# A decoder layer of 32 batches: one value run of sixteen heads a batch, new loop orders, rows of ones by transfers

## The reference

```python
# 1 self attention with a threshold
probs = softmax(x @ x.T / 16);  vac = where(probs < 0.01, probs, 0)
sparse = where(probs < 0.01, 0, probs);  sparse /= sparse.sum() + 1e-9
x = layernorm(x + sparse @ x + 0.01 * (vac.sum() broadcast over 256) @ W.T)
# 2 cross attention to 375 context rows, 16 heads of 16, masked keys at -1e15
q, k, v = x @ Wq + bq, ctx @ Wk + bk, ctx @ Wv + bv
x = layernorm(x + softmax(where(mask, -1e15, q k.T / 4)) v @ Wo + bo)
# 3 eight linear experts, the two of highest gate: sum over e of gate_e * x @ Wi[e] @ Wo[e]
x = layernorm(x + mixture)
```

## Time and profile before

| | |
|---|---|
| median of 3 runs | 750.13 us (749.94 to 752.53) |
| the profiled execution | 750.71 us, of which the span of instructions is 748.9 us |
| PE busy | 725.2 us (97%) |
| DVE busy | 663.0 us (89%) |
| ACT busy | 588.9 us (79%) |
| POOL busy | 213.4 us (28%) |
| DMA, mean | 148 GB/s; queue 1 takes 54.5% of 16 engines |
| the chain that ended last | PE 90%, DVE 4%, the rest 1% each or less |

### The profile page before, as it was taken

One profiled execution on the slowest core, in us unless ns is written; L12 is line 12 of the kernel. 1 busy time (PEld: TensorE's weight loads), 2 busy tenths in 40 slices (PEclk: granted clock), 3 DMA queues, 4 the chain that ended last, 5 costly groups with the idle time before them and its releaser, 6 DMA issues.

```text
span 748.9 us, 21146 instructions
## 1 busy us (share of the span) xinstructions
PE 725.2 (97%) x7250; PEld 655.5 (88%) x7250; DVE 663.0 (89%) x2608; ACT 588.9 (79%) x1435; POOL 213.4 (28%) x384
## 2 busy tenths in 40 slices
PE   5889999999999999999999999999999999999996
PEld 5769899999999989999999989999999988999875
DVE  4687889999999889999999989999999988898986
ACT  2368988888889898888888898888888898788740
POOL 2342332233332232333321333333123333232001
PEclk8998999999999999999999999999999999999999
DMA  8865754565555565555545566545556556544200
GB/s 252 233 185 138 189 156 123 152 159 149 155 154 137 143 177 153 153 156 139 158 135 149 157 169 159 159 134 150 139 151 164 149 150 174 154 130 128 63 17 28
DMA packets 75659, 110.84 MB, mean 148 GB/s; under 512 B 14224, under 2 KB 59168, under 8 KB 75552
## 3 DMA queue, kind: packets, MB, share of 16 engines
q1 hardware_dynamic: 75552, 109.49, 54.5%
HBM read 50.23 MB, written 18.35 MB: 92 GB/s over the span
## 4 chain that ended last, share of the span: by engine, by line
PE 90%; DVE 4%; DMA 1%; SPq 1%; ACT 1%; issue 1%; POOL 0%; POOLq 0%; DVEq 0%; ACTq 0%
PE psum L1633 20%; PE psum L1407 13%; PE psum L1441 11%; PE psum L1425 11%; PE psum L1500 4%; PE psum L1512 4%; PE psum L1487 4%; PE psum L1582 3%; PE psum L1545 3%; PE psum L1523 3%; PE psum L1534 3%; PE psum L1462 2%; PE psum L1563 2%; PE psum L1451 2%; SPq L393 1%; DVE scores_left L944 1%
## 5 line engine op out<-in xcount | busy, mean ns | idle before, releaser
L944 DVE CUSTOM_DVE_ANT_0 scores_left<-psum,mask_add 112x375 f32<-112x375 f32 x512 | 270.4, 542 | 22.3 <-PE psum L1407 15.7
L623 ACT ACTIVATE probsT<-psum 125x448 f32<-125x448 f32 x384 | 201.7, 537 | 17.4 <-PE psum L1425 13.4
L608 ACT ACTIVATE psum<-mask_u 125x448 f32<-125x448 uint8 x372 | 198.3, 541 | 3.7
L1407 PE MATMUL psum<-k_stack,q_stack 96*112 96x376 f32 x512 | 183.5, 366 | 1.5 <-DVE nmax L944 0.7
L1425 PE MATMUL psum<-q_stack,k_stack 97*125 97x224 f32 x768 | 148.5, 280 | 1.8 <-ACT psum L608 1.1
L1425 PEld LDWEIGHTS psum<-q_stack,k_stack 97*125 97x125 f32 x768 | 135.3, 189 | 12.5 <-ACT psum L608 2.5
L1176 DVE SCALAR_TENSOR_TENSOR late<-psum,gate,late 128x256 f32<-128x256 f32 x224 | 107.8, 481 | 19.6 <-PE psum L1633 10.8
L566 POOL TENSOR_TENSOR ctx_lo<-ctx_sb,ctx_hi 128x188 fp32r<-128x188 f32 x128 | 71.3, 587 | 129.6 <-ACT ctx_hi L731 129.6
L1407 PEld LDWEIGHTS psum<-k_stack,q_stack 96*112 96x112 f32 x512 | 89.6, 178 | 11.0 <-issue 5.6
L1633 PE MATMUL psum<-we_hi,x_hi 128*128 128x512 f32 x224 | 91.0, 406 | 0.5 <-DVE gate_nmax L1121 0.5
L1633 PE MATMUL psum<-we_hi,x_lo 128*128 128x512 f32 x224 | 88.4, 395 | 0.0
(11 more groups left out here) (169 smaller groups left out, 1627.9 us busy)
## 6 DMA issues: line engine op xcount, KB each, us to landing
k_stack<-k_hi SPq DMA_DIRECT2D x256, 94.0 KB, 2.6
q_stack<-q_scratch SPq DMA_DIRECT2D x96, 224.0 KB, 3.8
ctx_sb<-in_context_T SPq DMA_DIRECT2D x32, 376.0 KB, 3.6
k_stack<-k_lo SPq DMA_DIRECT2D x128, 94.0 KB, 2.5
q_scratch<-q_hi SPq DMA_DIRECT2D x32, 224.0 KB, 2.1
q_scratch<-q_lo SPq DMA_DIRECT2D x32, 224.0 KB, 2.0
xT<-in_x_T SPq DMA_DIRECT2D x32, 112.0 KB, 2.4
x_sb<-in_x SPq DMA_DIRECT2D x32, 112.0 KB, 2.9
```

Of the source, the lines that this page charges most:

```text
L608: nc.scalar.activation(psum[0:KP, ST_BANKS[i % 2], 0:4 * TOK].rearrange("p (h q) -> p h q", h=4), mask_u8[b % MASKS][:, KEYS + t * TOK:KEY ...
L623: nc.scalar.activation(probsT[:, place, i % KT, :], psum[0:KP, ST_BANKS[i % 2], 0:4 * TOK], ACT.Exp, scale=-1.0).then_inc(probs_ready, 1)
L944: nc.vector.tensor_tensor_reduce(scores_left[:, n % 2, :], psum[0:TOK, S_BANKS[n % 2], 0:KEYS], mask_add[b % 2][:, :], 1.0, 3.0e38, ALU.ad ...
L1407: nc.tensor.matmul(psum[0:TOK, S_BANKS[n % 2], 0:KEYS_EVEN], q_stack[s][0:96, pair, odd, c, :], k_stack[s][0:96, pair, c, :], start=True, ...
```

## The change

1. `weigh_values(b, 0, 1, 2, 3)`: one run of 48 matmuls a batch in place of two of 24; a wait for probabilities before each group of four heads. The last batch keeps two runs. `RING = GROUPS` (4), place = group.
2. `mx0` moves from between the first value run and `scores(8)` to behind `lg`, `att` and `scores(9)`, in front of `Sc`; `mx1` moves behind `aT`. `USES` follows.
3. DVE's `head` writes its sum over the logits in PSUM; `scores_left` is gone. `wv_sb`, `wo_sb`, `bv_wide` lie in `probsT`'s memory.
4. New orders in the loop of every engine: on DVE `expert(it-3, 7)` stands behind `cross`, `head` 12, 13 and 14 stand together, and so on. POOL makes `low_context` before the third layernorm's scalars.
5. The rows of ones are three DMAs of SP, from a row of `ones`, behind `load_mask(1)`; the memsets are gone.
6. Start: the wait for the constants stands at `PT(0)` and `open_blocks()`, the latter between `sum_values_bias()` and `K1(0)`. `qT(0)` waits for three loads only. End: `lg(27)` runs no idle matmuls, and the order has two for five.

```diff
-RING = 3
+RING = GROUPS
@@ head
-                    scores_left[:, n % 2, :], psum[0:TOK, S_BANKS[n % 2], 0:KEYS],
+                    psum[0:TOK, S_BANKS[n % 2], 0:KEYS], psum[0:TOK, S_BANKS[n % 2], 0:KEYS],
@@ weigh_values
-            def weigh_values(b, octet):
-                pe.wait_ge(probs_ready, BLOCKS * b + BLOCKS // OCTETS * (octet + 1))
-                for group in (2 * octet, 2 * octet + 1):
-                    place = (GROUPS * b + group) % RING
+            def weigh_values(b, *groups):
+                for group in groups:
+                    pe.wait_ge(probs_ready, BLOCKS * b + KT * (group + 1))
...
-                mm.then_inc(pv_done, 1)
+                    mm.then_inc(pv_done, 1)
@@ SP
+            def load_ones(k):
+                sp.wait_ge(setup_dve, 1)
+                sp.dma_start(k_stack[k][96:97, :, :, :].rearrange("o n c (x k) -> o (n c x) k", x=4).bitcast(fp32),
+                             ones[0:1, 0:KEYS_EVEN // 4].unsqueeze(1).broadcast_to([1, PAIRS * DC * 4, KEYS_EVEN // 4]))\
+                  .then_inc(weights_in, 16)
@@ POOL
-                nc.gpsimd.memset(k_stack[k][96:97, :, :, :].bitcast(fp32), 1.0).then_inc(setup_pool, 1)
@@ PE, prologue and end
-            Sc(0); open_blocks(); sum_attn_w(); PT(0); att(0); x1T_(0); Sc(1); qT(0); expert_product(0)
-            expert_product(1); PT(1); K0(0); sum_values_bias(); K1(0); V0(0); att(1); expert_product(2); V1(0)
+            Sc(0); sum_attn_w(); PT(0); att(0); x1T_(0); Sc(1); qT(0); expert_product(0); expert_product(1)
+            PT(1); K0(0); sum_values_bias(); open_blocks(); K1(0); V0(0); att(1); expert_product(2); V1(0); Sc(2)
...
             def lg(t):
-                if t == TILES - 1:
-                    run_idle(5)
...
-            weigh_values(31, 1); oT(31); m0(26); aT(31); m1(26); Wo(31); m2(26); m3(26); x2T_(31); run_idle(5); lg(27)
+            m3(26); x2T_(31); run_idle(2); lg(27); m0(27); m1(27); m2(27); m3(27)
```

More of the change, by code:

```diff
@@ new lines, in _ @@
+            self_max(4); self_nmax(4); sparse_r(3); y1(3); head(1, 11); stats1(3); head(1, 12); head(1, 13)
+            mom1(3); rsum(4); rden(0); o_norm(0); normalize_x1(3); head(1, 14); head(1, 15); self_p(4)
+            attn_rest(0); sparse(4); head(2, 0); head(2, 1); y2(0); vacuum(4); stats2(0); head(2, 2); mom2(0)
+            head(2, 3); k_lo1(3); vac_scaled(4); head(2, 4); head(2, 5); k_lo0(3); normalize_x2(0); sparse_den(4)
+            x_cas(4); sparse_r(4); head(2, 6); head(2, 7); x2_lo(0); head(2, 8); y1(4); head(2, 9); q_lo0(3)
@@ new lines, in _ @@
+                at(it - 1, rden)
+                at_tile(it - 2, gate_a)
+                at_tile(it - 2, gate_b)
+                at(it + 2, mom1)
+                at(it - 1, o_norm)
+                at_tile(it - 2, gate)
+                at(it + 3, vacuum)
+                at(it, head, 15)
+                at_tile(it - 3, normalize_out)
+                at_tile(it - 2, expert, 0)
+                at_tile(it - 2, expert, 1)
+                at(it - 1, attn_rest)
+                at_tile(it - 2, expert, 2)
@@ L1316, in _ @@
-            expert(22, 5); head(29, 3); vac_scaled(31); k_lo0(30); head(29, 4); normalize_x2(27); head(29, 5)
-            head(29, 6); k_lo1(30); expert(22, 6); expert(22, 7); q_lo0(30); head(29, 7); head(29, 8)
-            x_cas(31); x2_lo(27); stats3(22); sparse_r(31); head(29, 9); head(29, 10); y1(31); q_lo1(30)
-            head(29, 11); cross(23); mom3(22); gate_max(23); head(29, 12); gate_r(23); stats1(31)
-            head(29, 13); gate_p(23); mom1(31); head(29, 14); top_p(23); top_i(23); head(29, 15); top_f(23)
@@ L1326, in _ @@
[L1326 to L1327 removed]
+            normalize_out(21); rden(27); o_norm(27); top_f(22); gate_b(22); head(28, 12); head(28, 13); rsum(31)
+            attn_rest(27); gate_a(22); gate(22); self_p(31); expert(22, 0); head(28, 14); vacuum(31); sparse(31)
+            y2(27); head(28, 15); expert(22, 1); sparse_den(31); head(29, 0); normalize_x1(30); stats2(27)
@@ new lines, in _ @@
+            expert(22, 2); mom2(27); expert(22, 3); head(29, 1); head(29, 2); expert(22, 4); expert(22, 5)
+            head(29, 3); vac_scaled(31); k_lo0(30); head(29, 4); normalize_x2(27); head(29, 5); head(29, 6)
+            k_lo1(30); expert(22, 6); expert(22, 7); q_lo0(30); head(29, 7); head(29, 8); x_cas(31); x2_lo(27)
+            stats3(22); sparse_r(31); head(29, 9); head(29, 10); y1(31); q_lo1(30); head(29, 11); cross(23)
+            mom3(22); gate_max(23); head(29, 12); gate_r(23); stats1(31); head(29, 13); gate_p(23); mom1(31)
```

775 lines of the change are left out of this document (331 added, 444 removed), and 4 rows, old and new, of the table USES.

## The result

The kernel after takes 761.06 us (median of 4 runs, 758.12 to 767.75), the kernel before beside it 750.62. The ratio is 1.0148, with a 95% interval of 1.0111 to 1.0186. The forecast was 740.0 (735 to 748), so the sign was wrong. The profiled execution of after took 763.99, with a span of 761.9 (before: 750.71 and 748.9).

What follows compares the result with a forecast made beforehand. PE was taken as the bound, busy 100.00 of 100 us in mid-run. The sum was 750.71 - 6.8 + 0.8 - 3.0 + 0 - 1.2 = 740.5, less 0.6 for the median: 740.0 us, range 735 to 748.

Steps and rivals of the forecast that it cites:

- One value run, -6.8: PE's value matmuls: one run for two costs 2.61 for 2.83, saving 0.22 a batch in 31 batches, 6.8 us.
- The new orders, +0.8: Loops of all engines: waits of PE from thin margins cost 0.03 a batch, +0.8 us, between 0 and 0.3.
- The iterations without a tile keep their 1.8: Iterations without m0 to m3: PE's wait stays 1.8 us; less work between oT and Wo costs 0.2 four times.
- Ones by transfers, -3.0: Early in the kernel: memsets gone, PE's wait at `normalize_x1(2)` and half clock behind it go, -3.0 us, bounds 0 and -4.3.
- The end, -1.2: At lg(27): fewer idle matmuls let lg start at 735.35 instead of 736.57, -1.2 us, bound +3.
- The start, 0: Prologue: earlier PT(0) against `open_blocks` returning before K1(0), taken as 0, bounds -1.2 and +1.8.
- The moved transposes: mx0, mx1, PT, x2T and Sc on PE cost 0.10 each wherever they stand: 0, between -0.1 and 0.1 a batch.
- the PSUM write: DVE's head writing into the logits' bank: taken as 0, between -0.01 and 0.39 a head.
- the third rival: PSUM write costs DVE 0.06 a head, giving waits at scores 6, 10 and mx0, 0.1 to 0.2 a batch: 744; chance 0.10.
- The first: Rival: the order brings waits, mx0 and Sc hold PE 0.2 in each tile iteration: 746 (744.5 to 750); chance 0.17.
- The fourth: Rival: slower, DVE becomes the bound if reading and writing one bank halves the rate: 890; chance 0.05.

Runs made afterwards that it cites:

- old_order_two_runs: Kernel after with old loop orders, prologue, epilogue and bank order, and two value runs a batch; other changes stay: 749.55 us, ratio 0.9989.
- Kernel 6: Kernel after with TensorE's and ScalarE's whole prologue and epilogue from `old_order_two_runs`; the loop keeps the long run: 755.88 us, ratio 1.0087.
- kernel 3: `old_order_two_runs` with one value run of sixteen heads where the second run stood, mx0 at its old place: 781.56 us, ratio 1.0414.
- kernel 1: Kernel before with one edit, head writes its sum back into the logits' PSUM bank instead of scores_left: 751.44 us, ratio 1.0016.
- kernel 11: Kernel 6 with the old body of all engines and two runs in iterations without a tile and those behind them: 751.02 us, ratio 0.9994.
- kernel 10: Kernel 6 with, in iterations without a tile only, q_hi1 beside q_hi0, q_lo1 beside q_lo0, maxima sent behind low queries: 753.50 us, ratio 1.0042.
- kernel 4: `old_order_two_runs` with one swap in the loop, mx0 in front of the first value run, nothing merged: 778.04 us (one run).

## Why the prediction was wrong

*One value run, -6.8.* Right as the price of the run: 2.55 and three turns of 0.09 (in front of each run, behind the second), 2.82, went to 2.42 + 0.09 + 0.09 = 2.60, that is 0.22 a batch.

*The new orders, +0.8.* **This is the step that failed**, in three places.
- In an iteration with a tile I wrote 0.03 a batch for waits and got 0.19: from starts to starts Sc's first matmul takes 0.06 more and mx0 0.02 (`expert(t, 7)` and `gate_max`, the margin that I had put at 0.1 to 0.2), scores 14 takes 0.04 and scores 6 takes 0.07, where I had seen a margin of 0.3. So 0.22 became 0.03: 21.92 was forecast, 22.11 came, and over the 18 iterations nothing is left against the kernel before.
- "The iterations without a tile keep their 1.8", with 0.2 four times. They cost 4.8, 0.7 and 1.5 us more than before, of which some 3 are the clock. I walked the PE margins of an iteration with a tile, and of SP's queue I said that `neg_max_to_stack` "stands behind loads and key stacks whose releases are older". I never walked the way of the queries, q_hi1, q_lo1, two transfers, to scores(b+1, 0): in the new order q_lo1 comes 1.9 us later and the low queries leave SP 2.4 later.
- The prologue and the epilogue. The diff merges the runs and moves mx0 there too, without new orders round them, and I wrote nothing for it. Against `old_order_two_runs` it is 2.3 in front of K0(4), 2.3 from K0(29) to K0(31) and 4.1 behind, up to 1.7 of it clock. Kernel 6 gives about 5 of these back in median. Behind K0(31) PE in after has two waits that `old_order_two_runs` has not there. One is 0.6 at V2, for `nmaxT0`. The other is at lg(24), which needs `x2_lo(28)`; between x2T(28) and lg(24) the old epilogue has a first value run. PE's timeline:

```profile
697.08 0.28 PE L1553 MATMUL psum<-wr_parts,x_hi 128*128 128x16 f32 x1 [0.91 <-DVE x_lo L1082]
```


*What I missed at mx0 and at the ends:* I treated the first value run as work with a price, and asked what its turns cost. It was also the 1.28 us under which DVE's chain behind m3 ran out, and in the epilogue the cover of others. The iterations without a tile are another matter: mx0 comes no later there (7.6 behind K0, for 7.7 before), and what ends last is the way of the queries. The merge alone costs 32 us (kernel 3), and the new orders, which put mx0 behind that chain, win 20 of them back. My sum took the merge as the gain and the orders as a small cost on top.

*Ones by transfers, -3.0.* `normalize_x1(2)` fell to 0.41 and the clock is full from 54 to 60, as forecast. But K0(4) comes 2.0 earlier in `old_order_two_runs`, and kernel 1, with its memsets and a `normalize_x1(2)` of 2.78, has no half clock there either and reaches K0(4) at 92.9. So the cold six us of the earlier trace rows are not in every execution, and the median gained little of them. In after K0(4) stands at 95.1; kernel 6, which has two runs in the prologue, reaches it at 93.5.

*The end, -1.2.* Right: K0(31) to the end is 68.4 for 69.6 in `old_order_two_runs`. *The start, 0*: no run parts it from the ones; together they are the 2.0 above, against a start of kernel 1 that is as early.

*The moved transposes and the PSUM write.* Taken at 0 both. The 0.22 less the waits of 0.19 leaves 0.03, so the transposes and all else come out near 0; the write costs nothing that shows in the old order and some 0.04 for eight heads in the new one, where I had put it at 0 and, as the third rival, at 0.1 to 0.2 a batch. Its records are 16 + 59 = 75 ns longer, the start of the next one is 1 ns later. What the longer records cost is the wait of an engine that needs the head's end, as at scores 6. The Trainium skill (Perfetto Trace Analysis, section Optimizing Scalar/DVE Operations) gives about 60 ns of overhead on SBUF and about 125 on PSUM, as time in which the engine is busy. The distances, which would show that, differ by 1 ns; it is the records that are 75 ns longer.

*The rivals.* The first named the right sort of thing, waits that the order brings, but at mx0 and Sc alone, and stayed faster than before. The third named scores 6 as well, where the write does cost. The fourth had the right sign for the wrong reason: DVE was 94.5% busy (94.50 of 100 us in the window above), and set no pace. That a run which is removed takes a cover with it stood in no rival.

*The ladder of the ratios*, then: all but runs and orders 0.9989; the new body where a tile is made 0.9994 (kernel 11); also where none is 1.0087 (kernel 6); the long run in prologue and epilogue too 1.0148.

No version that does all the work beats the kernel before by more than its interval: `old_order_two_runs` comes nearest, 0.9989 (0.9971 to 1.0007).

What stays open: how much of the loss without a tile hangs on SP's queue, how much on the landings (4.0 and 4.5 us there, for medians of 2.8 and 4.2 over all batches). No experiment made the transfers smaller. Open too is the 2.3 between K0(29) and K0(31): the two runs of kernel 6 alone give back 0.6 of it, with the earlier queries of kernel 10 1.8, and no experiment shows how one hangs on the other.

## What to carry to other kernels

Before you merge or move a block of work on the engine that sets the pace, ask what waits ended under it. Here VectorE was late not by its load but by the chain that begins at the last result it was given. Walk the margins in every kind of iteration, in prologue and epilogue too, and along the queue that issues the transfers: the shortest iteration decides. When a change comes with new orders, price the bare change first; if it is ruinous alone, the orders are its repair and not a bonus.

## What the runs showed of the hardware

- A wait can cost more than its length. Round the wait of 1.65 the granted clock falls to 0.50 for 6.8 us. It need not: kernel 1 has a wait of 1.34 at the same place as the earlier trace rows and the clock stays at 1.00, and kernel 4 waits 0.96 in every iteration with a tile at a mean clock of 0.997. Over the four runs of after the mean clock of 0.997 and 0.999 goes with 758.1 us, 0.992 with 764.0 and 0.988 with 767.8; the spread of those four, 9.6, is three times that of the ten runs of `old_order_two_runs`, 3.3, whose clock stayed between 0.994 and 0.999.
- An issue of a transfer on SP can itself take long: the stack of queries at 261.25 took 1.95 us for 0.4 elsewhere, with the copy issued just before it; no run parts the cause.
- Reading and writing one PSUM bank in the head: 558 ns for 542, the accumulator read 142 for 83, but 468 ns from start to start for 467. The logits that need the head wait for the longer end: 0.25 for 0.19 at scores 6.
